# Second attention of a two-attention, two-expert-layer kernel: probabilities computed in the turned orientation instead of being transposed

## The reference

```python
q = (x @ Wq + bq).reshape(b, t, 16, 16)      # heads of 16 numbers
k = (x @ Wk + bk).reshape(b, t, 4, 16)       # four key heads, each for four query heads
v = (x @ Wv + bv).reshape(b, t, 4, 16)
q = q * cos + rotate_half(q) * sin           # the same for k
attn = jnp.einsum('bikgd,bjkd->bkgij', qg, k) * 16 ** -0.5
attn = jnp.where(causal, attn, jnp.finfo(dt).min)
p = jax.nn.softmax(attn.astype(jnp.float32), axis=-1).astype(dt)
out = jnp.einsum('bkgij,bjkd->bikgd', p, v).reshape(b, t, 256)
return out @ Wo
```

## Time and profile before

| | us |
|---|---|
| median of three runs | 960.7 |
| lowest, highest | 958.97, 961.12 |
| span of the profiled execution (first to last instruction) | 957.8 |
| second attention in it, 592.3 to 823.3 | 231.0 |
| busy, whole span: PE, DVE, ACT, POOL | 749.2, 617.6, 386.2, 253.0 |

### The profile page before, as it was taken

The page is one execution under the profiler, slowest core; times in us unless marked ns, Lnnn a source line. Parts: engine busy times, 40 slices in busy tenths (PEclk is TensorE's granted clock), DMA queues, the critical chain, the costliest instruction groups (busy, mean ns, idle before and its releaser), DMA issues. The chain is left out here.

```text
span 957.8 us, 13683 instructions
## 1 busy us (share of the span) xinstructions
PE 749.2 (78%) x4362; PEld 479.8 (50%) x4378; DVE 617.6 (64%) x1767; ACT 386.2 (40%) x1112; POOL 253.0 (26%) x268
## 2 busy tenths in 40 slices
PE   4689999999999998999886963466684756876970
PEld 2346555555565555778643542344444433633540
DVE  5767777777777775222495655687736786595643
ACT  1344555555445555210222200477815786222300
POOL 1522233333222330000145176200020000145175
PEclk8989999999999999999797985779976799996995
DMA  6000000100000000009803232000000000103343
GB/s 257 0 1 34 1 1 22 33 0 22 0 0 0 22 1 1 1 0 382 312 1 92 92 99 71 1 1 1 1 0 1 1 1 0 45 1 88 95 121 94
DMA packets 18387, 45.42 MB, mean 47 GB/s; under 512 B 4000, under 2 KB 12832, under 8 KB 17952
## 3 DMA queue, kind: packets, MB, share of 16 engines
q1 hardware_dynamic: 13440, 31.26, 8.9%
q0 software_dynamic: 4896, 13.51, 4.9%
HBM read 36.96 MB, written 7.34 MB: 46 GB/s over the span
## 5 line engine op out<-in xcount | busy, mean ns | idle before, releaser
L803 DVE TENSOR_REDUCE negmax<-ps 128x1 f32<-128x512 f32 (+3 forms) x128 | 56.9, 487 | 92.6 <-PE ps L1144 92.6
L1106 PE MATMUL ps<-w_qkv_a,xnT 128*128 (+2 forms) x256 | 97.3, 508 | 4.5 <-ACT nq L537 3.8
L567 ACT COPY pT<-ps 128x512 f32<-128x512 f32 (+1 forms) x96 | 43.2, 523 | 136.3 <-PE ps L1218 136.3
L1141 PE MATMUL ps<-kT,qT 128*128 128x512 f32 (+3 forms) x256 | 86.8, 461 | 1.0 <-DVE kT L774 1.0
L447 POOL TENSOR_TENSOR hrs<-hve,half 128x5 f32<-128x5 f32 x32 | 38.5, 1202 | 176.9 <-DVE hneg L789 176.8
L537 ACT ACTIVATE nq<-ps,hnm,hrs 128x128 f32<-128x128 f32 x160 | 59.2, 458 | 63.5 <-POOL hnm L449 63.5
L502 POOL DMA_INDIRECT xg<-y_rows,slot_of x64 | 64.3, 1005 | 57.3 <-DMA y_rows<-turn 37.4
L1156 PE MATMUL ps<-pT,vA 128*128 128x512 f32 (+3 forms) x256 | 76.0, 440 | 0.0
L853 DVE TENSOR_REDUCE negmax<-ps 128x1 f32<-128x512 f32 (+3 forms) x128 | 54.7, 484 | 31.2 <-PE ps L1272 31.2
L585 ACT ACTIVATE b_p<-ps,negmax 128x512 f32<-128x512 f32 (+3 forms) x128 | 66.9, 528 | 18.2 <-DVE negmax L853 17.7
L553 ACT ACTIVATE probs<-ps,negmax 128x512 f32<-128x512 f32 (+3 forms) x128 | 66.5, 558 | 10.0 <-DVE negmax L803 10.0
(11 more groups left out here) (156 smaller groups left out, 1551.6 us busy)
## 6 DMA issues: line engine op xcount, KB each, us to landing
w_down<-in_w_down SPq DMA_DIRECT2D x1, 4096.0 KB, 14.1
y_rows<-turn SPq DMA_DIRECT2D x32, 128.0 KB
w_qkv_a<-in_w_qkv SPq DMA_DIRECT2D x4, 768.0 KB, 5.4
w_gate<-in_w_gate SPq DMA_DIRECT2D x4, 512.0 KB, 3.3
w_o<-in_w_o SPq DMA_DIRECT2D x1, 2048.0 KB, 12.9
xn_rows<-xn SPq DMA_DIRECT2D x2, 1024.0 KB, 10.0
x_res<-in_x SPq DMA_DIRECT2D x2, 512.0 KB, 3.9
xg<-y_rows,slot_of POOLq DMA_INDIRECT x64, 2.8
```

Source lines behind the costliest of these rows:

```text
L803: op = dve.tensor_reduce(negmax[:, kp, i4:i4 + 1], wide[:, at:at + (i4 + 1) * P], AX, ALU.max, negate=True)
L1106: mm = pe.matmul(dst, xnT[:, k, col:col + P], w, start=(k == 0), stop=(k == KT - 1))
L1141: pe.matmul(wide[:, at:at + (i4 + 1) * P], qT[:, st, h, i4 * P:(i4 + 1) * P], kT[:, st, 0:(i4 + 1) * P], start=True, stop=False)
```

## The change

Only `small_heads` of each engine, its tiles and its constants change.

- q, k and v stay fp32. The splits, the stacks and their bf16 transposes go. Each token tile has 20 heads (16 of q, 4 of k) with 16 numbers in a slot of 32 columns (`b_qk`). The heads are reordered in the weights, so that four query heads that belong to four different key heads stand together. A transpose of four slots puts the four heads on partitions 0, 32, 64 and 96. Such four heads are a round: eight rounds, four for each batch.
- A round has two halves of two heads, and each half three jobs in one orientation (`IN_JOB`), as the banks had before. A job uses a pair of banks, one for each head. `scores` multiplies over 16 rows on the row group of each head, both in fp32, and then adds the mask to each by a bf16 matmul over all rows. VectorE takes the maxima of both heads in one instruction, and writes them negated into column 16 of the query slots.
- When a round's maxima are there, its query slots are transposed again (`shifted`). Row 16 of each slot is then the negative maximum, and row 16 of the keys is one. `turned_scores` multiplies over 17 rows with the keys as stationary operand: scores minus maximum, with keys on partitions and queries along the columns. ScalarE makes exponentials of both heads in one instruction, straight into `b_PT`, which is what the outputs need. Normalisation, transposes of probabilities and their copies go.
- Column 16 of v is one, so that row 16 of the outputs is the row sum. The outputs (`outputs`, four column groups, bank 6) are copied, transposed in bank 7, and divided by the sum there (`normalised`). Their projection has 2 instead of 4 blocks of rows.
- Score jobs and turned jobs alternate over three pairs of banks, the turned ones nine jobs behind. Bank 7 is shared by the small steps; `in_bank_7` says which has it at a step. Batch 1's projection, its rotation and batch 0's output projection are such steps, inside the loop. The loop is unrolled.
- POOL sets the unused columns of `b_qk` to zero ahead of its first cosine part. The preparation goes one tile at a time.

The core of the diff:

```diff
-SPLITS = 8
+BREP = BH // BKV
+QK = BH + BKV
+PAD = 32
+ROUNDS = B * BREP
+JOBS = 6 * ROUNDS
+BEHIND = 9
...
+IN_JOB = [[(3, 0)], [(2, 0), (0, 3 * P)], [(1, 0)]]
+
+KEYS_IN_JOB = [[(0, 0)], [(1, 0), (3, 3 * P)], [(2, 0)]]
+
+PART_AT = [0, 2 * S, 4 * S]
+
+PART_OF = {0: (0, S, 0), 1: (1, S, 0), 3: (1, S, 3 * P), 2: (2, 2 * P, 0)}
+
+
+RING = [job for v in range(JOBS + BEHIND) for job in (("scores", v), ("turned", v - BEHIND))
+        if 0 <= job[1] < JOBS]
+RING_AT = {job: n for n, job in enumerate(RING)}
...
+def in_bank_7(v):
+
+    r, c = v // 6, v % 6
+    if c == 0 and 0 <= r - 3 < ROUNDS:
+        return "outputs", r - 3
+    if c == 1 and 0 <= r - 1 < ROUNDS:
+        return "shifted", r - 1
+    if c == 4 and r + 1 < ROUNDS:
+        return "queries", r + 1
+    if c in (2, 3) and r < ST // 2:
+        return "project", ST + 2 * r + c - 2
+    if (r, c) == (2, 3):
+        return "keys", 1
+    if r == BREP + 2 and c in (2, 3):
+        return "heads", c - 2
+    if (r, c) in ((BREP + 2, 5), (BREP + 3, 2)):
+        return "add", r - BREP - 2
+    return None
+
+
+STEPS = 6 * (ROUNDS + 2) + 1
+BANK_7 = [("queries", 0)] + [u for u in map(in_bank_7, range(STEPS)) if u]
 
 
...
+        bqk = sb("b_qk", [P, B, ST, QK, PAD], F32, low)
+        bPT = sb("b_PT", [P, 3, HALF_P], F32, low)
+        bmT = sb("b_mT", [P, 2, S], F32, low)
+        bv = sb("b_v", [P, B, ST, BKV, PAD], F32, low)
+        boT = sb("b_oT", [P, S], F32, low)
+        bqkv = sb("b_qkv", [P, 2, BCOLS], F32, low)
+        bsn = sb("b_sn", [P, QK, BD], F32, low)
+        brs = sb("b_rs", [P, ST, BKV], F32, low)
...
+        bkT = xn[:, 0:4].rearrange("p n d -> p (n d)").rearrange("p (b s) -> p b s", s=S)
+        bqT = xn[:, 4:8].rearrange("p n d -> p (n d)").rearrange("p (b s) -> p b s", s=S)
+        bo = xnT[:, 0].rearrange("p (n d) -> p n d", d=D)
+        bwT = xnT[:, 1].rearrange("p (k s) -> p k s", s=S)
...
+                pool.memset(bqk[:, :, :, :, BD:PAD], 0.0).then_inc(b_pads, 1)
+                pool.wait_ge(b_pads, 1)
+                pool.memset(bqk[:, :, :, BH:QK, BD], 1.0).then_inc(b_pads, 1)
...
+                    pool.wait_ge(b_qkv, m + 1)
+                    pool.tensor_tensor(bqk[:, m // ST, m % ST, :, 0:BD],
+                                       bqkv[:, m % 2, 0:QW + KW].rearrange("p (h d) -> p h d", d=BD),
+                                       bcos[:, m % ST:m % ST + 1].broadcast_to([P, QK, BD]), ALU.mult).then_inc(b_cosp, 1)
+                    if m == 1:
+                        pool.memset(bv[:, :, :, :, BD:PAD], 0.0).then_inc(b_vpads, 1)
+                        pool.wait_ge(b_vpads, 1)
+                        pool.memset(bv[:, :, :, :, BD], 1.0).then_inc(b_vpads, 1)
...
+                    if 0 <= v - BEHIND < JOBS:
+
+                        u = v - BEHIND
+                        half, c = u // 3, u % 3
+                        bank = pair_of("turned", u)
+                        w = S if c < 2 else 2 * P
+                        act.wait_ge(b_st, u + 1)
+                        if half >= 3 and c == 0:
+                            act.wait_ge(b_pv, (half - 3) // 2 + 1)
+                        nc.scalar.activation(bPT[:, half % 3, PART_AT[c]:PART_AT[c] + 2 * w].rearrange("p (u w) -> p u w", w=w),
+                                             ps[:, bank:bank + 2, 0:w], ACT.Exp, scale=BD ** -0.5).then_inc(b_exp, 1)
+                    if v % 6 == 5 and 0 <= v // 6 - 2 < ROUNDS:
+
+                        act.wait_ge(b_pv, v // 6 - 1)
+                        nc.scalar.copy(boT[:], ps[:, 6, :]).then_inc(b_oT, 1)
...
+                def biased(m, bank):
+
+                    dve.wait_ge(b_mm, m + 1)
+                    if m >= 2:
+                        dve.wait_ge(b_cosp, m - 1)
+                        dve.wait_ge(b_v, m - 1)
+                    dve.tensor_tensor(bqkv[:, m % 2], ps[:, bank, 0:BCOLS], bb[:], ALU.add).then_inc(b_qkv, 1)
+                    dve.wait_ge(b_qkv, m + 1)
+                    if m >= 1:
+                        dve.wait_ge(b_rot, m)
+                    dve.tensor_tensor(bsn[:].rearrange("p h (u d) -> p h u d", u=2),
+                                      bqkv[:, m % 2, 0:QW + KW].rearrange("p (h u d) -> p h u d", u=2, d=BD // 2)[:, :, ::-1],
+                                      bsin[:, m % ST:m % ST + 1].rearrange("p o (u d) -> p o u d", u=2)
+                                      .broadcast_to([P, QK, 2, BD // 2]), ALU.mult).then_inc(b_sinp, 1)
+
+                def rotated(m):
+                    dve.wait_ge(b_cosp, m + 1)
+                    dve.wait_ge(b_sinp, m + 1)
+                    at = bqk[:, m // ST, m % ST, :, 0:BD]
+                    dve.tensor_tensor(at, at, bsn[:], ALU.add).then_inc(b_rot, 1)
+
+                def maxima(v):
+
+                    r, half, c = v // 6, v % 6 // 3, v % 3
+                    b, head = r // BREP, r % BREP * BKV + 2 * half
+                    bank = pair_of("scores", v)
+                    dve.wait_ge(b_s, v + 1)
+                    for n, at in IN_JOB[c]:
+                        op = dve.tensor_reduce(bqk[:, b, n, head:head + 2, BD], ps[:, bank:bank + 2, at:at + (n + 1) * P],
+                                               AX, ALU.max, negate=True)
+                    op.then_inc(b_max, 1)
+
+                def normalised(r):
+
+                    j = r % BREP
+                    heads = ps[:, 7, :].rearrange("p (n i c) -> p n i c", n=ST, c=PAD)
+                    dve.wait_ge(b_oturned, r + 1)
+                    if r >= 1:
+                        dve.wait_ge(b_norm, r)
+                    dve.reciprocal(brs[:], heads[:, :, :, BD]).then_inc(b_rinv, 1)
+                    dve.wait_ge(b_rinv, r + 1)
+                    dve.tensor_tensor(bo[:, :, j * BKV * BD:(j + 1) * BKV * BD].rearrange("p n (i d) -> p n i d", d=BD),
+                                      heads[:, :, :, 0:BD], brs[:].unsqueeze(3).broadcast_to([P, ST, BKV, BD]),
+                                      ALU.mult).then_inc(b_norm, 1)
...
+                def pair_free(kind, v):
+
+                    if RING_AT[kind, v] >= 3:
+                        before, u = RING[RING_AT[kind, v] - 3]
+                        pe.wait_ge(b_max if before == "scores" else b_exp, u + 1)
+
+                def bank_7_free(kind, k):
+
+                    at = BANK_7.index((kind, k))
+                    if at > 0:
+                        before, u = BANK_7[at - 1]
+                        taken = {"outputs": b_norm, "shifted": b_mT, "queries": b_qT, "project": b_qkv, "keys": b_kT,
+                                 "heads": b_wT, "add": x_added}[before]
+                        pe.wait_ge(taken, 2 * NT + 2 * u + 2 if before == "add" else u + 1)
+
+                def scores(v):
+
+                    r, half, c = v // 6, v % 6 // 3, v % 3
+                    bank = pair_of("scores", v)
+                    if v % 6 == 0:
+                        pe.wait_ge(b_qT, r + 1)
+                        pe.wait_ge(b_kT, r // BREP + 1)
+                    pair_free("scores", v)
+                    for n, at in IN_JOB[c]:
+                        for u in range(2):
+                            rows = slice((2 * half + u) * PAD, (2 * half + u) * PAD + BD)
+                            pe.matmul(ps[:, bank + u, at:at + (n + 1) * P], bqT[rows, r % 2, n * P:(n + 1) * P],
+                                      bkT[rows, r // BREP, 0:(n + 1) * P], start=True, stop=False)
+                        for u in range(2):
+                            mm = pe.matmul(ps[:, bank + u, at + n * P:at + (n + 1) * P], identb[:], maskb[:], start=False, stop=True)
+                    mm.then_inc(b_s, 1)
+
+                def turned_scores(v):
+
+                    r, half, c = v // 6, v % 6 // 3, v % 3
+                    bank = pair_of("turned", v)
+                    if v % 6 == 0:
+                        pe.wait_ge(b_mT, r + 1)
+                    pair_free("turned", v)
+                    for m, at in KEYS_IN_JOB[c]:
+                        for u in range(2):
+                            rows = slice((2 * half + u) * PAD, (2 * half + u) * PAD + BD + 1)
+                            pe.matmul(ps[:, bank + u, at:at + S - m * P], bkT[rows, r // BREP, m * P:(m + 1) * P],
+                                      bmT[rows, r % 2, m * P:S], start=True, stop=False)
+                        for u in range(2):
+                            mm = pe.matmul(ps[:, bank + u, at:at + P], maskb[:], identb[:], start=False, stop=True)
+                    mm.then_inc(b_st, 1)
+
+                def outputs(r, m):
+                    for i in range(BKV):
+                        c, w, at = PART_OF[m]
+                        at += PART_AT[c] + i % 2 * w
+                        mm = pe.matmul(ps[i * PAD:(i + 1) * PAD, 6, m * P:S], bv[:, r // BREP, m, i],
+                                       bPT[:, (2 * r + i // 2) % 3, at:at + S - m * P], start=(m == 0), stop=(m == 2))
+                    return mm
+
...
```

(56 more changed lines are left out.)

381 lines of the change are left out of this document (118 added, 263 removed).

## The result

The changed kernel takes 1038.8 us (median of 4 runs, 1032.5 to 1043.3); the kernel before took 959.8 beside it (958.5 to 961.1). The ratio is 1.082, with a 95% interval of 1.079 to 1.086. It is slower by 8%, where 924 had been forecast.

A forecast was written before the change was run, and what follows sets the result against it. TensorE was to become the bound of the second attention's loop (161 us of work, 167 with waits and start). Preparation -11.7, loop -24.8 and end +0.1 gave -36.4: span 921.4, plus 2.9 makes 924 us; range 886 to 993.

The forecast's parts named there:

- The step that failed: Second attention's loop: 512-column fp32 score passes take 0.43 us, a pair of heads the price of one; 68.8 us.
- the clock falls: Rival on the second attention's loop: passes run 1.69 times as long at a lower clock; +83, 1007 us, chance 0.07.
- Row groups side by side: Score products in the loop: two heads on two row groups and two banks cost the price of one.
- the row groups take turns: Rival on score products: two heads cost two passes one behind another; +68.8, 993 us, chance 0.12.
- half overlap: Rival on score products: program-order starts make three pass times for a pair, not two; +34.4, 959 us, chance 0.10.
- The rest of the sum: TensorE's other loop terms: masks 14.1, tiling changes 41.0, outputs 17.2, transposes 11.4, projections 5.1 and 3.4 us.
- Change of tiling: Loop, between row groups and full-height products: 152 round trips at 0.27 us, 41.0 us in all.
- upper end of +17: Loop: fp32 weight loads queueing across row groups, 0.5 us a group of 32; up to +17, none added.
- no drain: Rival on the loop: no drain between row groups and masks, or loads hidden; up to -41, 883 us, chance 0.13.
- Preparation: Before the loop: tile by tile, first scores at 611 against 622.7, -11.7 us; batch 1's preparation hides under TensorE.
- The end: From the last output matmul to the last add: 8.5 us against 8.4 before, +0.1.
- Banks and bank 7: Loop: 4 us added for bank 7 waits; rival of VectorE or ScalarE holding banks, about +20, chance 0.03.

The follow-up runs named there:

- 64-row run: Changed kernel with each head's score products over 64 rows instead of 16 or 17, so two heads' scores are added up: 924.4 us, ratio 0.966.

## Why the prediction was wrong, point by point

- **The step that failed: the clock.** The sum priced every score pass at 0.43 us, the pace of the earlier trace rows, which were four column groups of products over all 128 rows at the upper level. It took their side-by-side working over to row groups, and the clock with it. The clock did not follow: 0.50 for most of the loop, and 0.54 on average. The rival *the clock falls* was the case, and had 0.07. The argument against it was "no idle time, and the 0.84 of before fell after waits". The windows of after, 40.00 busy of 40.00 at 0.50, show that a lack of waits is not enough. The Trainium skill (TensorE: Matmul & The Clock Gate, Part 1, What's actually happening) says that the clock follows how busy the array has been; by busy time alone this loop would be at the upper level, and by that rule it would have taken the 169 us of the 64-row run. The measurement decides: with as many passes and the array as busy, the rows that the score products address made the difference, and the profile's busy share doesn't show them.
- **The rival's size.** It was priced at +83 (120 us of passes x 0.69, the ratio of the earlier trace rows) and cost +110 (276.7 - 167). Masks, transposes and the changes of tiling slow down too, and they were left out. And the ratio was too small, since the 3.99 us of the earlier trace rows were only in part at the lower level:

```profile
758.76:762.75 3.99, 3.99 (x34) 1.38 (x34) 2.82 (x10) 2.14 (x8) 0.00 (x0) 0.57 0.02 4
```

  The 512-column tile went from 1.27 to 2.33 us, 1.83 times and not 1.69. All 161 us at 1.83 would be +134; the loop was not at 0.50 for all of its length.
- **Row groups side by side: right.** At the upper clock the four passes of two heads take 1.06 us to the masks side by side and 1.77 one behind another; two pass times are 0.86 and three would be 1.29. So *the row groups take turns* (0.12) and *half overlap* (0.10) are out. Without masks even four went together.
- **The rest of the sum: right at the upper clock, as a sum.** The loop was forecast at 167 and took 168.7 with 64 rows and 170.7 with the keys kept twice; the span 921.4, against 924.1 and 925.8. Score passes, masks, changes of tiling, outputs and the small products hold together; they were not measured one by one.
- **Change of tiling: sum right, parts otherwise.** 0.27 was taken as 0.12 on the way in and 0.15 on the way out. In the 64-row run a 512-column tile takes 1.27, which is 0.86 of passes, 0.11 of masks and 0.30 besides. Of that, 0.20 lies between the first pass and the masks (1.06 between 689.57 and 690.63, for 0.86 of passes), and 0.10 between the last mask and the next pass. With all 128 rows four passes take 1.77, 0.44 each, so that nearly all of the 0.20 goes. It belongs to the change and not to each pass: with the masks after both tiles, passes of two tiles take 1.07 for 0.86 of passes (691.02 to 692.09), the same 0.2 for twice as many. So weight loads that wait behind each other, kept as an upper end of +17, were not a term of their own. That a change of mode costs time, as the Trainium skill says (TensorEngine Tiling (Array Packing), Key Properties), is borne out: where one is gone, a job is 0.30 us shorter. The rival *no drain* (0.13) is out.
- **Preparation: nearly right.** First scores at 611.6 against 611, in part by luck: the stages ahead ended 0.6 us earlier (the first projection starts at 591.74, not 592.31), and from there to the first scores it takes 19.9 us where 18.7 had been forecast. VectorE came to the first bias at 599.85 and not at 598.75. Padding went from 596.6 to 598.8, and the last sum ended at 608.9 against 609. Batch 1's preparation is hidden.
- **The end: right.** 8.3 us (888.3 to 896.6) against 8.5.
- **Banks and bank 7: right in kind.** TensorE hardly waits for the pairs of banks (0.7 us ahead of L1288, 0.0 ahead of L1304), and for bank 7 it waits as had been thought, output transposes for ScalarE's copy: 2.5 us here and 3.3 in the 64-row run, of the 4 that were added. VectorE's maxima wait for TensorE (170.4 us on L896) and so do ScalarE's exponentials (136.4 on L642).
- **The chances.** 0.22 for slower was mostly on the row groups, which the columns of the earlier trace rows had nearly settled, and too little on the clock, on which no row bore: nothing in the trace of before was a long stretch of passes on few rows. The range ended at 993, under the 1007 of its own rival, and left out the case that came, which went 32 us beyond even that.

## What to carry to other kernels

Before a contraction over few rows takes the place of one over many, ask what clock it will be granted, and not only how many passes it has; price the lower clock on everything in that stretch, masks and transposes included. If the rows beside the operand can hold zeros, address them: with 32 rows it cost no instruction, and took 94 us off here. Look at the stretches at both ends as well, where one kind of product stands alone. Put products that use row groups together, and full-height ones behind them, since each change there and back costs about 0.3 us.

## What the runs showed of the hardware that had not been expected

- The granted clock depends on the rows that products address, even where they hold zeros. For the same columns it was 0.50 to 0.54 over the middle 200 us with pairs of 16 and 17 rows (0.50 exactly from 680 to 800, without a pause), 1.00 in the steady loop with pairs of 32 but 0.50 and 0.51 at its two ends, and 1.00 with pairs of 64 or with 128 after some 4 to 9 us at the start.
- Passes in four row groups, issued as two pairs by different lines of the program into different banks, start within 0.01 us of each other; with masks between the pairs, in the changed kernel, the second pair starts behind the masks (703.79 and 704.12).
- A change from full height to row groups and back costs 0.30 us at the upper clock, 0.2 of it before the full-height product starts and 0.1 after it. It is the same for two passes of each head and for four; passes over row groups with no change between them (two tiles, 1.07 us for 0.86 of passes) add nothing.
